# Reordering the front of a fused convolution, dense and low-rank kernel: taps summed earlier, half of A in other PSUM banks, shared factors loaded earlier

## The reference, cut to what matters

```python
# x: (64, 64, 1024)  cond: (64, 128)  side: (64,)
y = conv1d(x, weight, groups=4, padding=4)          # 9 taps, 64 channels in 4 groups of 16
y = y + einsum('nd,od->no', cond, c_weight)[:, :, None] + side[None, :, None]
# gate: (8, 16) mixes 16 LoRAs of rank 32 into one per block of 8 samples
A_eff = einsum('bn,nri->bri', gate, lora_A)         # (8, 32, 1024)
B_eff = einsum('bn,nor->bor', gate, lora_B)         # (8, 1024, 32)
out = y @ kernel + bias                             # kernel: (1024, 1024)
out = out + (y @ A_eff^T) @ B_eff^T                 # per block of 8 samples
out = out + (y @ A_shared^T) @ B_shared^T           # shared factors, rank 32
return x + out
```

## Time and profile before

| what | value |
|---|---|
| median of 3 runs | 498.38 us (498.1 to 499.8) |
| the profiled execution | 499.44 us |
| its span, first to last instruction | 497.6 us |
| PE busy | 487.3 us (98%) |
| DVE, ACT, POOL busy | 319.3, 167.2, 271.2 us |
| PE's share of the chain that ended last | 94% |
| mean granted TensorE clock | 0.997 of full |

### The profile page before, as it was taken

One profiled execution on the slowest core, in us unless ns is written; L12 is line 12 of the kernel. 1 busy time (PEld: TensorE's weight loads), 2 busy tenths in 40 slices (PEclk: granted clock), 3 DMA queues, 4 the chain that ended last, 5 costly groups with the idle time before them and its releaser, 6 DMA issues.

```text
span 497.6 us, 6737 instructions
## 1 busy us (share of the span) xinstructions
PE 487.3 (98%) x2417; PEld 402.7 (81%) x2417; DVE 319.3 (64%) x368; ACT 167.2 (34%) x205; POOL 271.2 (55%) x153
## 2 busy tenths in 40 slices
PE   7899999999999999999999999999999999999997
PEld 6576988888888888888888888888888888888886
DVE  5656584969757594857937596675939388473402
ACT  3655433442333143322424133431524224241100
POOL 1789955872928265570928338372756519392200
PEclk9899999999999999999999999999999999999999
DMA  8952657542624163340725236240634313251302
GB/s 254 421 209 78 226 146 197 227 154 71 238 55 122 59 207 130 77 123 10 257 74 123 75 109 216 48 126 38 236 101 111 90 31 83 67 123 67 95 32 84
DMA packets 16733, 64.56 MB, mean 130 GB/s; under 512 B 1520, under 2 KB 1968, under 8 KB 15824
## 3 DMA queue, kind: packets, MB, share of 16 engines
q1 hardware_dynamic: 16640, 64.35, 41.8%
q10 hardware_dynamic: 80, 0.04, 0.1%
HBM read 45.10 MB, written 18.87 MB: 129 GB/s over the span
## 4 chain that ended last, share of the span: by engine, by line
PE 94%; DMA 2%; DVE 1%; POOL 1%; SPq 1%; issue 0%; ACT 0%; DVEq 0%; POOLq 0%
PE main L922 69%; PE rank L935 6%; PE main L927 3%; PE conv L864 3%; PE conv L866 3%; PE conv L865 3%; DMA sh_in<-in_shared 2%; PE conv L840 2%; PE spare L866 1%; PE spare L865 1%; PE spare L864 1%; PE main L910 1%; PE conv L902 1%; DVE w_raw L679 1%; POOL as_st L340 0%; POOL bs_st L344 0%
## 5 line engine op out<-in xcount | busy, mean ns | idle before, releaser
L922 PE MATMUL main<-w_hi,y_hi 128*128 128x512 f32 x504 | 156.1, 391 | 0.7 <-DVE a_eff L683 0.4
L922 PE MATMUL main<-w_lo,y_hi 128*128 128x512 f32 x504 | 154.9, 389 | 0.0
L922 PE MATMUL main<-w_hi,y_lo 128*128 128x512 f32 x504 | 154.8, 389 | 0.0
L377 POOL TENSOR_TENSOR y_lo<-y_stage,y_hi 128x512 fp32r<-128x512 f32 x56 | 93.3, 1687 | 34.3 <-ACT y_hi L480 34.3
L922 PEld LDWEIGHTS main<-w_lo,y_hi 128*128 128x128 f32 x504 | 94.6, 188 | 20.2
L922 PEld LDWEIGHTS main<-w_hi,y_lo 128*128 128x128 f32 x504 | 94.6, 188 | 19.9
L922 PEld LDWEIGHTS main<-w_hi,y_hi 128*128 128x128 f32 x504 | 93.6, 188 | 20.6 <-DVE a_eff L683 0.9
L357 POOL TENSOR_TENSOR xd_lo<-xd,xd_hi 128x512 fp32r<-128x512 f32 x28 | 40.3, 1439 | 100.3 <-ACT xd_hi L492 100.3
L359 POOL TENSOR_TENSOR x_lo<-x_tr,x_hi 128x1024 fp32r<-128x1024 f32 x28 | 82.3, 2938 | 15.7 <-ACT x_hi L494 15.7
L494 ACT ACTIVATE x_hi<-x_tr 128x1024 fp32r<-128x1024 f32 x28 | 57.7, 2061 | 27.6 <-DVE x_tr L649 27.6
L480 ACT ACTIVATE y_hi<-y_stage 128x512 fp32r<-128x512 f32 x56 | 35.5, 633 | 91.8 <-DVE y_stage L667 91.8
(11 more groups left out here) (102 smaller groups left out, 503.2 us busy)
## 6 DMA issues: line engine op xcount, KB each, us to landing
res<-in_x SPq DMA_DIRECT2D x32, 512.0 KB
out<-res SPq DMA_DIRECT2D x31, 512.0 KB
x_in<-in_x_rows SPq DMA_DIRECT2D x6, 2048.0 KB, 12.8
w_raw<-in_L_ffn_kernel SPq DMA_DIRECT2D x4, 1024.0 KB, 17.5
b_cur<-b_scratch SPq DMA_DIRECT2D x21, 128.0 KB, 3.1
x_tr<-in_x_first SPq DMA_DIRECT2D x1, 2064.0 KB, 8.8
la<-in_L_ffn_lora_A SPq DMA_DIRECT2D x4, 512.0 KB, 9.8
lb<-in_L_ffn_lora_B SPq DMA_DIRECT2D x1, 2048.0 KB, 25.4
```

Source lines behind the costliest of these rows:

```text
L377: nc.gpsimd.tensor_tensor(y_parity(y_lo, h, t, e), y_staged(e), y_parity(y_hi, h, t, e).bitcast(F32), ALU.subtract).then_inc(ylo_done, 1)
L922: mm(main[t][:, n * 512:(n + 1) * 512], lhs, rhs[:, k, n * 512:(n + 1) * 512], start=k == 0 and first, stop=False)
```

## The change

Five edits, all in the order or place of work; no operation is added or removed.

```diff
 def a_out(q):
-    return main[1][:, (q % 2) * 512:...]
+    return main[1 - q // 2][:, (q % 2) * 512:...]          # q = 2, 3 now in main[0]
 sync:
     load_la(sp, 0)
     load_first(sp, 0)
-    load_la(sp, 1)
     sp.dma_start(sh_in[0:2 * R, :], shared).then_inc(shared_in, 16)
-    for q in range(2, RQ):
+    for q in range(1, RQ):
         load_la(sp, q)
 scalar:
+    act.wait_ge(tlo_done, 2)
+    nc.scalar.activation(t01_raw ..., main[0][:, 512:1024] ..., ACT.Copy).then_inc(t01_copied, 1)
     x_first_high(0)
     act.wait_ge(shared_in, 16)
     shared_high(0)
     shared_high(1)
-    act.wait_ge(tlo_done, 2)
-    nc.scalar.activation(t01_raw ..., main[0][:, 512:1024] ..., ACT.Copy).then_inc(t01_copied, 1)
     ...
     w_high(0)
     w_high(1)
+    x_first_high(1)
     w_high(2)
-    x_first_high(1)
 vector:
     t_low(0)
     t_low(1)
+    dve.wait_ge(t01_copied, 1)
+    nc.vector.tensor_tensor(t01_raw ..., main[0][:, 0:512] ..., t01_raw ..., ALU.add).then_inc(t01_sum, 1)
     x_first_low(0)
     a_turn(0)
     dve.wait_ge(ctx_done, 1)
     y_tile(0, 0, 0, FIRST, first=True)
-    dve.wait_ge(t01_copied, 1)
-    nc.vector.tensor_tensor(t01_raw ..., main[0][:, 0:512] ..., t01_raw ..., ALU.add).then_inc(t01_sum, 1)
+    y_tile(0, 0, 1, FIRST, first=True)
     a_turn(1)
-    y_tile(0, 0, 1, FIRST, first=True)
+    a_turn(2)
     w_add(0)
     w_add(1)
-    a_turn(2)
-    w_add(2)
-    w_add(3)
     a_turn(3)
-    for m in range(4, 8):
+    for m in range(2, 6):
         w_add(m)
     x_first_low(1)
+    w_add(6)
+    w_add(7)
     y_tile(0, 0, 2, FIRST, first=True)
 tensor, mix_a(q):
     if q < 2:
         pe.wait_ge(gmix_done, 1)
     else:
-        pe.wait_ge(a_done, q - 1)
+        pe.wait_ge(t01_sum, 1)
 tensor, chunk(k):
-    if k == 0 and t == 1 and product == 0:
+    if k == 0 and t == 0 and product == 0:
         pe.wait_ge(a_done, RQ)
```

More of the change, by code:

```diff
@@ L195, in a_out @@
         def a_out(q):
-            return main[1][:, (q % 2) * 512:(q % 2 + 1) * 512].rearrange("p (b k m) -> p b k m", b=2, m=32)
+            return main[1 - q // 2][:, (q % 2) * 512:(q % 2 + 1) * 512].rearrange("p (b k m) -> p b k m", b=2, m=32)
         def load_first(eng, half):
@@ L462, in x_first_high @@
                     nc.scalar.activation(x_part(x_hi[:, t], half), x_raw(t, *x_half(half)), ACT.Copy).then_inc(x0_hi, 1)
+            act.wait_ge(tlo_done, 2)
+            nc.scalar.activation(t01_raw[:, :, :, :].rearrange("p g s c -> p s g c"),
+                                 main[0][:, 512:1024].rearrange("p (s g c) -> p s g c", s=J, g=G), ACT.Copy).then_inc(t01_copied, 1)
             x_first_high(0)
@@ L467, in _ @@
             shared_high(1)
-            act.wait_ge(tlo_done, 2)
-            nc.scalar.activation(t01_raw[:, :, :, :].rearrange("p g s c -> p s g c"),
-                                 main[0][:, 512:1024].rearrange("p (s g c) -> p s g c", s=J, g=G), ACT.Copy).then_inc(t01_copied, 1)
             def y_high_first(u, i, order):
@@ L696, in _ @@
             t_low(1)
+            dve.wait_ge(t01_copied, 1)
+            nc.vector.tensor_tensor(t01_raw[:, :, :, :].rearrange("p g s c -> p s g c"),
+                                    main[0][:, 0:512].rearrange("p (s g c) -> p s g c", s=J, g=G),
+                                    t01_raw[:, :, :, :].rearrange("p g s c -> p s g c"), ALU.add).then_inc(t01_sum, 1)
             x_first_low(0)
@@ L700, in _ @@
             y_tile(0, 0, 0, FIRST, first=True)
-            dve.wait_ge(t01_copied, 1)
-            nc.vector.tensor_tensor(t01_raw[:, :, :, :].rearrange("p g s c -> p s g c"),
-                                    main[0][:, 0:512].rearrange("p (s g c) -> p s g c", s=J, g=G),
-                                    t01_raw[:, :, :, :].rearrange("p g s c -> p s g c"), ALU.add).then_inc(t01_sum, 1)
+            y_tile(0, 0, 1, FIRST, first=True)
             a_turn(1)
-            y_tile(0, 0, 1, FIRST, first=True)
+            a_turn(2)
             w_add(0)
             w_add(1)
-            a_turn(2)
-            w_add(2)
-            w_add(3)
             a_turn(3)
-            for m in range(4, 8):
+            for m in range(2, 6):
                 w_add(m)
             x_first_low(1)
+            w_add(6)
+            w_add(7)
             y_tile(0, 0, 2, FIRST, first=True)
```

## The result

The changed kernel took 497.02 us (median of 8 runs, 495.57 to 497.80), the kernel before, run beside it, 499.09 us (8 runs, 497.80 to 500.75): a ratio of 0.9949, with a 95% interval of 0.9932 to 0.9965. By the ratio that is 2.5 us, or 0.5%, faster; the two medians differ by 2.1 us; 3.0 us (0.6%) was forecast. The forecast value was 495.4; the median lies 1.6 us above it, just inside the range given, 494.6 to 497.1. Some 0.7 us of the 1.6 are not the change's: the kernel before measured 499.09 in 8 runs, and the forecast started from 498.38 in 3. The profiled execution took 497.13 us with a span of 495.3, against 497.6 before: 2.3 us less.

The account below looks back on a forecast made before the run. PE was taken to bound the kernel, with POOL's chain meeting it at chunk(4). Chunk(4) starts 3.6 us earlier, waits 0.5 us for w_low(4) and ends 3.0 us earlier: 495.4 us from 498.38, range 494.6 to 497.1.

Parts of the forecast that it names:

- What bounds it: Front, first 60 us: PE runs without a gap after 33.4 us, so time saved there is saved at the end.
- POOL hold PE by 0.5 us: At chunk(4): PE wants w_low(4) at 42.85, POOL ends it at 43.3, so PE waits 0.5 us.
- the cover of 0.9 us at chunk(4): Kernel before: chunk(4)'s last four matmuls start at 46.42, w_low(4) is done at 45.50, so PE is 0.9 us behind POOL.
- Shared ahead, as_lo at 13.35: Load queue and POOL: shared lands near 11, as_lo starts at 13.35 in place of 14.27, 0.92 us gained.
- Kernel part 0 as the new wait of w_add(0): On DVE: w_add(0) waits for kernel part 0, landing at 19.54; w_add(1) ends at 20.85, 1.3 us gained.
- merge(4) 1.8 us earlier: On PE behind chunk(0): merge(4) starts at 25.36 in place of 27.15, 1.8 us gained.
- PE from merge(4) to chunk(4): PE goes from merge(4) at 25.36 through to 41.0; chunk(4) starts 3.6 us earlier than 44.59.
- POOL from w_low(2) to w_low(4): POOL: w_low(2) starts at 28.3, 0.35 us of idle goes, x_low_second(0) starts 2.15 us earlier, w_low(4) ends at 43.3.
- The clock: PE's idle from 17.7 to 19.38, shortened to 0.75 us: the sum lets PE run at 2.4 GHz.
- The first rival: Clock falls into chunk(0) and chunk(1): merge(4) 2.1 us later, gain shrinks to 0.9, 497.5; chance 0.11.
- The tests it set itself: Profile signs, such as with_a(0) at 55.2; wrong if POOL idles from 28.3 to 43 or PE waits after 50.
- w_low(2) later than 29: On POOL: sign that the prediction is wrong; w_low(2) was forecast to start at 28.3.

Follow-up runs that it names:

- late_half: The kernel before with only the late edits: x_first_high(1) ahead of w_high(2), x_first_low(1) ahead of w_add(6) and w_add(7); 497.33 us, ratio 0.9966.
- after_again: The changed kernel once more, unaltered, measured beside other variants; 496.73 us, ratio 0.9956 to the kernel before.
- filler: The changed kernel with two more identity matmuls behind mix_a(0), in PE's idle time; 496.20 us, ratio 0.9932 to the kernel before.
- merge_early: The changed kernel with merge(4) and merge(5) inside chunk(0), ahead of the product that waits for w_low(0); 496.43 us, ratio 0.9947.
- xh_old: The changed kernel with only ACT's x_first_high(1) moved back behind w_high(2), DVE's new order kept; 498.62 us, ratio 0.9975.
- early_half: The changed kernel without its late edits: x_first_high(1) again behind w_high(2), x_first_low(1) again behind w_add(7); 498.02 us, ratio 0.9980.
- sp_only: The kernel before with only the new load order, shared ahead of A's second quarter; 499.33 us, ratio 0.9999.
- sp_old: The changed kernel with the old load order, A's second quarter ahead of shared; 496.67 us, ratio 0.9940.
- x_late: The changed kernel with x's first half issued behind shared and A's second quarter; 498.60 us, ratio 0.9995.
- x_ahead: merge_filler with three identity matmuls, x's first half loaded before A's first quarter, first convolutions before mix_a(0), taps' copy and A's first turn later; 496.20 us, ratio 0.9944.
- merge_filler: The changed kernel with merge(4) and merge(5) ahead of chunk(0)'s last product and two identity matmuls behind mix_a(0); 496.02 us, ratio 0.9944.

## Why the prediction was right, and where its steps were not

- *What bounds it.* Right in that the front is decided by chunk(4), where PE's chain and POOL's meet: in all 14 profiles the span is the start of chunk(4)'s last product plus 451.3 to 451.5 us, and PE doesn't wait after it. Which of the two comes last there is another matter:

| kernel | chunk(4)'s first matmul | its last product | w_low(4) done | PE held |
|---|---|---|---|---|
| before | 44.42 | 46.26 | 45.50 | no |
| late_half | 42.27 | 44.17 | 44.11 | 0.06 |
| changed | 41.94 | 43.83 | 43.75 | 0.05 |
| after_again | 41.45 | 43.41 | 43.32 | 0.12 |
| filler | 40.49 | 42.44 | 42.35 | 0.11 |
| merge_early | 41.34 | 43.18 | 42.68 | no |
| xh_old | 43.95 | 45.79 | 45.39 | no |

(Held is what the stretch takes over the unheld 1.84.) The prediction had POOL hold PE by 0.5 us there. Measured were 0.05 to 0.12: PE was 1.1 us later than forecast (chunk(4) at 42.11 in the view of the earlier trace rows, forecast 41.0), POOL 0.45 (w_low(4) done at 43.75, forecast 43.3). So PE's own order limits the changed kernel about as much as POOL does. A small error lies under it: the cover of 0.9 us at chunk(4) was taken from the chain's view (46.42); PE's timeline has 46.26, so it was 0.75.
- *Shared ahead, as_lo at 13.35.* Mis-sized. It named ACT's rounding and POOL's x_lo as what would come last, which is right, but took both at the times of one execution in which x landed early. In the changed kernel's profile as_lo started at 14.17, in filler, with x at 9.39, at 13.33. In filler the rest of the chain also came as forecast: merge(0) 18.48 (forecast 18.46), w_low(2) 27.95 (28.3). In the kernel before, as_lo waited for shared, at 13.03, and x could come up to 1.4 us later at no cost to it (ACT's idle time ahead of 13.06); in the changed kernel nothing covers x's landing any more.
- *Kernel part 0 as the new wait of w_add(0).* Wrong. It landed at 17.8 in the changed kernel (issued at 5.07, 12.7 us), not at 19.54, and w_add(0), at 20.55, waited for nothing but its turn behind a_turn(2). A landing read from one profile of a full queue is good to about a us or two.
- *merge(4) 1.8 us earlier.* Measured 0.7 in the changed kernel's profile, 1.2 in after_again's (25.99). Of the forecast 1.8, 0.9 was merge(0)'s and 0.9 came between merge(0) and merge(4). The second half came (1.05 us in the changed kernel, 1.24 in after_again), the first did not: merge(0) was 0.37 and 0.08 us later than before. Only in filler, with x early, is it there (0.90). The whole early part is worth 1.0 us in the timed runs (early_half), not the 1.8 that the sum carried forward.
- *PE from merge(4) to chunk(4).* Right: 15.6 us forecast, 15.5 measured. The text speaks of a wait of 1.1 us that goes, but the sum takes off the full 1.8.
- *POOL from w_low(2) to w_low(4).* Mis-sized: 12.7 us forecast, 11.95 measured. The term that was left out is bias_lo, 1.03 us before and 0.31 after. It brought POOL level with PE; beyond the forecast wait of 0.5 us it could give nothing.
- *The clock.* The row was read as a promise that idle time of 1.6 us ahead of the first convolution does no harm. The first rival was right that a fall would come, and wrong about the place: it came in the first convolutions (1.2 GHz, about 12 to 15.4 us), not in chunk(0), and cost about 0.5 us.
- *The tests it set itself.* "w_low(2) later than 29" came true (29.43), and with it POOL's idle time after 28.3; they rightly marked the early chain as wrong. No clock of 0.50 showed between 22 and 30, and PE did not wait after 50. with_a(0) came at 55.78 in place of 55.2.

So 3.0 was forecast and 2.1 to 2.5 measured: PE arrived at chunk(4) 1.1 us late, all of it in the early part, and got back the 0.5 us that it was to wait there for POOL, by a shortening of bias_lo that the prediction had not seen. That the median stayed in the range is in part luck.

## What to carry to other kernels

When an operation is moved on one engine, list what stands behind the instruction that waits for it on the other engines, and which operations it then runs beside; here that was worth more, by the medians, than the moves the change was named for. A transfer's landing in a full queue is a range and not a number: where every later step hangs on it with slope one, as on x's first half here, take two or three landings before building a sum to a tenth of a us. Where two engines meet, look at who arrives last and by how much, before saying which of them sets the end. And an end that moves by half a per cent is best followed in the profiles by one time stamp that all variants share (here the start of chunk(4)'s last product), beside the medians, which carry the noise of every run.

## What the runs showed of the hardware that was not expected

- **DVE and POOL hold each other up when both read only SBUF.** DVE's x_first_low(1) reads two tiles in SBUF; it took 1.08 us while POOL was idle (changed kernel, from 28.18) and 2.26 us when it began 1.4 us before POOL's w_low(2) ended (xh_old). In all seven profiles where it began under an operation of POOL it ended 0.82 to 0.87 us after that operation, however long before it had begun (0.4 to 1.4 us): it looks blocked until POOL is through. POOL's bias_lo, 16x64 elements, took 0.31 us alone and 0.99 to 1.03 us in the four profiles where it began under that DVE operation (before, early_half, sp_only, xh_old); in each it ended 0.13 to 0.15 us after DVE did (32.57 and 32.44 in xh_old). DVE's w_adds, with one operand in PSUM, took 0.65 to 0.69 us beside POOL all the time. The Trainium skill, "SBUF — State Buffer", Who interferes with whom, says that a tensor_tensor of VectorE with both inputs in SBUF contends with GpSimd's reads, one of the two blocking and not sharing; these rows agree. The prediction did not look for it.
- **How long PE idles did not tell whether the clock falls.** The granted clock fell from 2.4 to 1.2 GHz (0.50) after 1.9, 2.1, 2.2 and 3.1 us of idle ahead of the first convolution (sp_only, sp_old, xh_old, the changed kernel) and during 3.4 us of it (x_late), and did not after 2.4 and 2.7 (after_again, merge_early).
- **The granted clock that the profile shows is not safe before its first change.** It reads 1.00 through the first 13 us of x_ahead and of filler. But the same matmul of the identity, 128x256, took 634 ns in x_ahead at 7.2 to 9.4 us (as at 1.5 to 3.0 us in every profile) and 379 ns in filler at 9.0 to 9.7. In merge_filler, whose program is filler's up to there, it took 634 ns again (9.1 to 10.6), with 1.00 shown. X_ahead and filler:

```profile
L940 PE MATMUL conv<-ident x6: 634/634/793, 7.2 to 9.4; 128*128 128x256 f32 x6
```

```profile
L941 PE MATMUL conv<-ident x4: 379/379/483, 9.0 to 9.7; 128*128 128x256 f32 x4
```

The convolution behind it in x_ahead ran slowly too: four matmuls took 1.05 us from 10.73 on, as they did in the changed kernel at a granted clock of 0.50, where 0.63 is usual at 1.00. From 12.34 on they took 0.65. So PE most likely ran at 1.2 GHz until about 12 us there, though no row of the clock says so:

```profile
10.00:11.00 1.00, 1.00 (x7) 1.00 (x6) 0.57 (x2) 0.84 (x2) 1.00 (x1) 1.00 0.98 385
```

What lets ACT start on x's first half at 9.2 us in one execution and at 10.4 in the next, with the same loads ahead of it, stays open.
